# QR of P on GpSimd: reflectors in pairs in place of one at a time

## The reference

```python
U, _ = jnp.linalg.qr(P)                 # P: (144, 64), the same for all sequences
R = _rotation(cond, W, b)               # expm of a 64x64 skew matrix, one per sequence
z = jnp.einsum('btn,nd->btd', x, U)
z_rot = jnp.einsum('btd,bde->bte', z, R)
x_rot = x + jnp.einsum('btd,nd->btn', z_rot - z, U)
```

## Time and profile before

| | |
|---|---|
| median of three executions | 1263.58 us |
| profiled execution, span from first to last instruction | 1267.7 us |
| TensorE busy | 1194.4 us, 94% |
| VectorE busy | 910.0 us, 72% |
| ScalarE busy | 788.0 us, 62% |
| GpSimd busy | 749.6 us, 59%, 2230 instructions |
| mean granted TensorE clock | 0.974 |

### The profile page before, as it was taken

How to read it: one execution, slowest core, us unless ns; L and a number is a source line. 1 busy time by engine, 2 the same in 40 slices (tenths; PEclk the granted TensorE clock), 3 DMA queues, 4 the chain that set the end, 5 groups by cost and what they waited for, 6 DMA issues and landing times.

```text
span 1267.7 us, 35439 instructions
## 1 busy us (share of the span) xinstructions
PE 1194.4 (94%) x12778; PEld 949.3 (75%) x12778; DVE 910.0 (72%) x2496; ACT 788.0 (62%) x1809; POOL 749.6 (59%) x2230
## 2 busy tenths in 40 slices
PE   4899999899899999999999999999899999999997
PEld 2677777688676777778888888887777777777775
DVE  6799999766579999965575555554679999955432
ACT  3589898756479898963342333233379888874531
POOL 5656656666656656566676666667777777740000
PEclk9999999999979999999999999999969999989997
DMA  6321121242531121130210111120121111101130
GB/s 171 62 19 19 18 23 16 48 97 33 107 67 20 15 21 16 21 57 5 16 14 5 16 15 7 13 44 20 35 43 27 31 35 33 23 6 20 19 66 28
DMA packets 50319, 42.82 MB, mean 34 GB/s; under 512 B 8455, under 2 KB 45754, under 8 KB 49717
## 3 DMA queue, kind: packets, MB, share of 16 engines
q1 hardware_dynamic: 45884, 29.91, 10.9%
q0 software_dynamic: 3488, 8.52, 8.4%
q10 hardware_dynamic: 780, 2.17, 0.5%
HBM read 33.86 MB, written 3.03 MB: 29 GB/s over the span
## 4 chain that ended last, share of the span: by engine, by line
PE 82%; DVE 13%; issue 4%; ACT 2%; DMA 0%; SPq 0%; ACTq 0%; DVEq 0%
PE PS L1678 18%; PE PSA L1399 15%; PE PSA L1456 8%; PE PS L1480 8%; PE PS L1441 7%; PE PS L1399 6%; DVE BIG L544 3%; PE PSB L1651 2%; PE PS L1511 2%; PE PS L1501 2%; PE PS L1512 2%; PE PSB L1463 1%; PE PS L1506 1%; PE PS L1491 1%; DVE xh L508 1%
## 5 line engine op out<-in xcount | busy, mean ns | idle before, releaser
L1255 ACT ACTIVATE BIG<-PSA 128x512 f32<-128x512 f32 (+1 forms) x224 | 132.0, 593 | 264.1 <-PE PSA L1399 264.0
L1678 PE MATMUL PS<-w,BIG 128*128 128x144 f32 (+1 forms) x1920 | 254.7, 287 | 7.6 <-DVE BIG L818 4.1
L544 DVE TENSOR_REDUCE BIG<-PSA 128x8 f32<-128x1024 f32 x192 | 234.1, 1219 | 31.9 <-PE PSA L1456 29.9
L1678 PEld LDWEIGHTS PS<-w,BIG 128*128 128x128 f32 (+1 forms) x1920 | 245.1, 190 | 15.6 <-DVE BIG L818 4.9
L1124 ACT ACTIVATE BIG<-PSB 128x1024 f32<-128x1024 f32 x192 | 195.5, 1018 | 20.5 <-PE PSB L1463 20.3
L1456 PEld LDWEIGHTS PSA<-KK,Q 32*128 32x128 f32 x1536 | 109.9, 196 | 57.8 <-issue 41.0
L1456 PE MATMUL PSA<-KK,Q 32*128 32x128 f32 x1536 | 135.1, 294 | 14.9 <-DVE BIG L544 4.7
L1441 PE MATMUL PS<-K,qt 128*128 128x128 f32 x768 | 127.3, 293 | 10.4 <-DVE qt L539 4.8
L1463 PE MATMUL PSB<-Q,KK 32*128 32x128 f32 x1536 | 133.9, 293 | 0.0
L1480 PE MATMUL PS<-BIG,VA 128*32 128x128 f32 x3072 | 128.5, 287 | 1.1 <-DVE col L419 1.1
L1893 POOL MEMSET qprod<- 128x2 f32 x63 | 6.2, 99 | 203.0 <-DMA VB<-QA 203.0
(11 more groups left out here) (307 smaller groups left out, 2955.8 us busy)
## 6 DMA issues: line engine op xcount, KB each, us to landing
gate<-gates SPq DMA_DIRECT2D x96, 72.0 KB, 2.9
mgate<-gates SPq DMA_DIRECT2D x96, 72.0 KB, 2.7
VB<-skew POOLq DMA_DIRECT2D x16, 288.0 KB, 3.7
X<-in_x SPq DMA_DIRECT2D x4, 576.0 KB, 11.4
out<-X SPq DMA_DIRECT2D x8, 288.0 KB, 3.6
BIG<-in_skew_w SPq DMA_DIRECT2D x2, 1024.0 KB
w<-in_w SPq DMA_DIRECT2D x1, 1440.0 KB, 11.4
BIG<-in_wqkv SPq DMA_DIRECT2D x2, 584.0 KB
```

Source lines behind the costliest of these rows:

```text
L544: V.tensor_reduce(nmax.rearrange("p (s w) -> p s w", w=HP)[:, 2 * a:2 * a + 2, 3 * HD:3 * HD + G], PSA[:, :].rearrange("p (r g k) -> p r g ...
L1255: S.activation(hm[0:rows, slot, :], PS[(par * FTOT[l] + j) % 2][0:rows, :], gelu).then_inc(gelu_done, 1)
L1678: last = mm(o, hm[0:rows, slot, s * 128:(s + 1) * 128], w2[0:rows, FT * e + k, :], start=(k == 0), stop=(k == FT - 1))
```

## The change

Reflectors are made two at a time. `reflect_first(k)` broadcasts rows k and k + 1 together (two DMAs, one wait) into two buffers that lie behind `QA`, so that an instruction can run over two or three of the rows at once. It forms three sums in one tree of the same eight levels: QA times row k, row k times itself, row k + 1 times row k. With them it applies reflector k to `QA` and to the broadcast copy of row k + 1 in one subtraction. `reflect_second(k + 1)` then needs no broadcast: the copy is up to date. The one-column instructions are regrouped to run over two or three neighbouring scalars, and small values (TINY) stand where zeros stood. On the way back `unreflect` takes two rows: three sums in one tree (UT times either row, row times row), a correction for the second factor, and two subtractions. The tree lives in two buffers instead of seven. The rest of the kernel is as it was.

```diff
+            def add_up(product, n):
+                a = product
+                for size, t in ((72, qtree), (36, qtwo), (18, qtree), (9, qtwo), (4, qtree), (2, qtwo[:, 32:64]), (1, qtree)):
+                    t = t[:, 0:n * size].rearrange("p (n c) -> p n c", n=n)
+                    link(R.tensor_tensor(t, a[:, :, 0:size], a[:, :, size:2 * size], ALU.add))
...
+                link(R.tensor_tensor(qs[:, 0:n].rearrange("p (n o) -> p n o", o=1), a, nine[:, :, 8:9], ALU.add))
...
             def broadcast(k):
-                rows_in[k % 2] += 16
-                row = QA[k:k + 1, k:C].rearrange("p (o n) -> p o n", o=1).broadcast_to([1, 128, C - k])
-                pool.dma_start(QB[k % 2][:, k:C], row).then_inc(q_row[k % 2], 16)
+                for j in range(2):
+                    row = QA[k + j:k + j + 1, k:C].rearrange("p (o n) -> p o n", o=1).broadcast_to([1, 128, C - k])
+                    pool.dma_start(reach[:, 1 + j, k:C], row).then_inc(q_row, 16)
...
+            def signed_root(k):
+                link(R.tensor_tensor(norm, sq, qc[:, 0:1], ALU.pow))
+                link(R.tensor_scalar(qsn[:, k:k + 1], side, -1.0, norm, ALU.add, ALU.mult))
...
+            def kept_factors(k):
+                R.tensor_scalar(qtau[:, k:k + 1], first[:, 1:2], SMALL, qtau[:, k:k + 1], ALU.is_gt, ALU.mult)
+                R.tensor_scalar(qtau[:, k + 1:k + 2], second[:, 1:2], SMALL, qtau[:, k + 1:k + 2], ALU.is_gt, ALU.mult)
...
+            def mixed(k, to, n, step):
+                span = slice(0, 3, step)
+                link(R.tensor_tensor(to, reach[:, span, k], qsn[:, k:k + 1].broadcast_to([128, n]), ALU.mult))
+                link(R.tensor_tensor(to, to, qs[:, 0:n], ALU.add))
+                R.tensor_tensor(to[:, 0:1], to[:, 0:1], qmask[:, k:k + 1], ALU.mult)
+                link(R.tensor_tensor(qtau[:, k:k + 1], to[:, 1:2], qc[:, 1:2], ALU.pow))
...
+            def reflect_first(k):
                 broadcast(k)
                 if k:
-                    R.memset(qprod[:, :, k - 1:k], 0.0)
...
+                    kept_factors(k - 2)
+                    R.memset(products[:, :, k - 2:k], TINY)
+                pool.wait_ge(q_row, 32 * (k // 2 + 1))
+                v = reach[:, 1, :]
+                R.tensor_tensor(products[:, 1:3, k:C], reach[:, 1:3, k:C],
+                                v[:, k:C].rearrange("p (o n) -> p o n", o=1).broadcast_to([128, 2, C - k]), ALU.mult)
+                link(R.tensor_tensor(products[:, 0, k:C], QA[:, k:C], v[:, k:C], ALU.mult))
...
+                signs(k, v)
+                add_up(products, 3)
+                signed_root(k)
+                mixed(k, first, 3, 1)
+                at = slice(k + 1, C)
+                R.tensor_scalar(products[:, 0, at], v[:, at], first[:, 0:1], qtau[:, k:k + 1], ALU.mult, ALU.mult)
+                link(R.tensor_scalar(products[:, 2, at], v[:, at], first[:, 2:3], qtau[:, k:k + 1], ALU.mult, ALU.mult))
+                link(R.tensor_tensor(reach[:, 0:3:2, at], reach[:, 0:3:2, at], products[:, 0:3:2, at], ALU.subtract))
...
+            def reflect_second(k):
+                v = reach[:, 2, :]
+                R.memset(products[:, 0:2, k - 1:k], TINY)
+                R.tensor_tensor(products[:, 1, k:C], v[:, k:C], v[:, k:C], ALU.mult)
+                link(R.tensor_tensor(products[:, 0, k:C], QA[:, k:C], v[:, k:C], ALU.mult))
+                signs(k, v)
+                add_up(products[:, 0:2], 2)
+                signed_root(k)
+                mixed(k, second, 2, 2)
...
+            for k in range(0, RD, 2):
+                reflect_first(k)
+                if k == RD - 2:
+                    pool.wait_ge(sk_ld, 32)
+                    pool.dma_start(v_rows, QA[0:RD, :]).then_inc(v_st, 16)
+                reflect_second(k + 1)
...
+            def unreflect(k, vb, j):
+                v = vb[:, j * C:(j + 2) * C].rearrange("p (n c) -> p n c", n=2)
+                at, n = slice(k, C), C - k
+                R.tensor_tensor(back[:, 0:2, at], v[:, :, at], UT[:, at].rearrange("p (o n) -> p o n", o=1)
+                                .broadcast_to([128, 2, n]), ALU.mult)
+                link(R.tensor_tensor(back[:, 2, at], v[:, 0, at], v[:, 1, at], ALU.mult))
+                add_up(back, 3)
+                link(R.tensor_scalar(side, qs[:, 2:3], qs[:, 1:2], qtau[:, k + 1:k + 2], ALU.mult, ALU.mult))
+                R.tensor_scalar(back[:, 1, at], v[:, 1, at], qs[:, 1:2], qtau[:, k + 1:k + 2], ALU.mult, ALU.mult)
+                link(R.tensor_tensor(norm, qs[:, 0:1], side, ALU.subtract))
+                link(R.tensor_scalar(back[:, 0, at], v[:, 0, at], norm, qtau[:, k:k + 1], ALU.mult, ALU.mult))
+                link(R.tensor_tensor(UT[:, at], UT[:, at], back[:, 1, at], ALU.subtract))
+                link(R.tensor_tensor(UT[:, at], UT[:, at], back[:, 0, at], ALU.subtract))
```

More of the change, by code:

```diff
@@ L43 @@
 K_N = K_LOW + NE * NE
-FWD, BWD = 15, 6
+TINY, SMALL = 1e-37, 1e-30
 RADD = bass.bass_isa.ReduceOp.add
@@ L1855, in _ @@
             pool.wait_ge(q_at, 1)
-            steps, rows_in = [2], [0, 0]
+            steps = [2]
             def link(ins):
@@ L1884, in _ @@
[L1884 to L1889, removed]
+            link(R.tensor_scalar(qmask, K[:, K_SGN:K_SGN + RD], 0.0, None, ALU.is_lt))
+            qtwo = QU[:, :, :].rearrange("p n c -> p (n c)")
+            def add_up(product, n):
[3 more added lines that the diff above has]
+                    link(R.tensor_tensor(t, a[:, :, 0:size], a[:, :, size:2 * size], ALU.add))
+                    if size == 9:
+                        nine = t
+                    a = t
+                link(R.tensor_tensor(qs[:, 0:n].rearrange("p (n o) -> p n o", o=1), a, nine[:, :, 8:9], ALU.add))
@@ new lines, in _ @@
+            reach = qrows[:, 2 * C:5 * C].rearrange("p (n c) -> p n c", n=3)
+            products = VB[1][:, 0:3 * C].rearrange("p (n c) -> p n c", n=3)
+            sq, side, norm, first, second = qs[:, 1:2], qs[:, 3:4], qs[:, 4:5], qs[:, 5:8], qs[:, 8:10]
+            def broadcast(k):
+                for j in range(2):
+                    row = QA[k + j:k + j + 1, k:C].rearrange("p (o n) -> p o n", o=1).broadcast_to([1, 128, C - k])
+                    pool.dma_start(reach[:, 1 + j, k:C], row).then_inc(q_row, 16)
@@ new lines, in reflect_first @@
+                link(R.tensor_tensor(reach[:, 0:3:2, at], reach[:, 0:3:2, at], products[:, 0:3:2, at], ALU.subtract))
[8 more added lines that the diff above has]
+                mixed(k, second, 2, 2)
+                if k == RD - 1:
+                    kept_factors(k - 1)
+                    return
+                at = slice(k + 1, C)
+                link(R.tensor_scalar(products[:, 0, at], v[:, at], second[:, 0:1], qtau[:, k:k + 1], ALU.mult, ALU.mult))
+                link(R.tensor_tensor(QA[:, at], QA[:, at], products[:, 0, at], ALU.subtract))
@@ L1929, in _ @@
+            NG = RD // VG
+            pool.wait_ge(v_st, 16)
             load_group(NG - 1)
             load_group(NG - 2)
+            link(R.memset(qrows[:, 0:3 * C], 0.0))
             for g in reversed(range(NG)):
@@ L1933, in _ @@
                 pool.wait_ge(v_ld[g % 2], 16 * ((NG - 1 - g) // 2 + 1))
-                link(R.tensor_copy(vb[:, k0:k0 + (VG - 1) * (C + 1) + 1:C + 1], qdiag[:, k0:k0 + VG]))
-                for j in reversed(range(VG)):
-                    unreflect(k0 + j, vb[:, j * C:(j + 1) * C])
+                pivots = vb[:, k0:k0 + (VG - 1) * (C + 1) + 1:C + 1]
+                R.memset(vb[:, C + k0:C + k0 + 2 * (C + 1) + 1:2 * (C + 1)], 0.0)
+                link(R.tensor_tensor(pivots, pivots, qsn[:, k0:k0 + VG], ALU.add))
+                for j in reversed(range(0, VG, 2)):
+                    unreflect(k0 + j, vb, j)
                 if g >= 2:
```

58 lines of the change are left out of this document (16 added, 42 removed).

## The result

The kernel after takes 1275.65 us in the median, the kernel before 1266.62 in the runs beside it (nine each; the 1263.58 that the prediction is set against was the median of the first three). The ratio is 1.0075, 95% interval 1.0048 to 1.0101: about 9 us slower. The profiled execution took 1280.35 us with a span of 1278.2.

The account below looks back on a forecast made before the run. The prediction took the TensorE and VectorE chain to bound the kernel, not GpSimd. VectorE's burden, 3.8 us saved and 1.9 added, netted -1.9; half reaching the end gave -1.0 from 1263.58, so 1262.6 us, range 1258.4 to 1267.

Parts of the forecast that it names:

- What bounds the kernel: Chain of TensorE 82% and VectorE 13%, without GpSimd; U is ready 15.3 us before it is read.
- The price of the pairs: GpSimd's QR: 21.7 us a pair forward against 25.9, 7.3 back plus 1.5 a group; U ready near 970 us.
- the bounds given: Last write of UT: right if between 900 and 1040 us.
- What the earlier end is worth: VectorE's burden in the three attentions: 3.8 us saved, 1.9 added, net -1.9; about half reaches the end, -1.0 us.
- a factor of 1.3: First two attentions: burden follows squared GpSimd durations over time, 2.9 in 12.97 to 6.3 in 21.7; 6.2 us grows by 1.9.
- The read part is the "slower" rival's rule: First two attentions: only duration above 0.2 us blocks, squares grow by 2.2; +7.4 against -3.8 us, 1267.2; chance 0.13.
- the credit: Third attention: GpSimd works only 45 of 200 us, so 3.8 of VectorE's 4.8 us burden go.
- The step from excess to time: About half of VectorE's time change reaches the end, as VectorE waits for TensorE at times.
- The faster one: Passage from third attention to its MLP: TensorE's clock doesn't fall, 7 us of work take 3.5; 1257.6 us, chance 0.22.
- The range: Whole kernel: 1258.4 to 1267 us, from near the faster rival to the slower one.
- the added fall of the clock: First passage, with the slower rival: a further fall of the clock would add 3.4 us.
- The 0.2% that the prediction said a measurement can tell: Whole kernel: a measurement can tell about 0.2%, 2.5 us, from no change.

Follow-up runs that it names:

- The streams: In place of the QR, GpSimd repeats one instruction of fixed width: products of 16, 72, 144 or 288 columns, or memsets; ratios to before 0.9971 to 1.1765.
- the single forward part and the new way back: Kernel after with the forward part one reflector at a time, in the new buffers, the way back still in pairs; ratio to before 1.0089.
- 72 columns: No QR; in its place GpSimd does 2150 products of 72 columns from two SBUF inputs; ratio to before 1.0081.
- the 144 column stream: No QR; in its place GpSimd does 1600 products of 144 columns from two SBUF inputs; ratio to before 1.0501.
- the wide stream: No QR; in its place GpSimd does 1130 products of 288 columns from two SBUF inputs; ratio to before 1.1765.
- the pause: Kernel after with one GpSimd wait, 63 us long, ahead of group 9 of the way back; ratio to before 1.0064.
- the kernel with all split: Kernel after with row instructions over 100 columns halved, tree levels in pieces of at most 72 columns, trees shrunken; 1266.0 us against before's 1265.55, ratio 0.9993.
- the one with new forward part and single back: Kernel after with the way back one reflector at a time, in the new buffers, the forward part still in pairs; ratio to before 1.0045.

## Why the prediction was wrong

**What bounds the kernel: right.** U was not waited for, before or after, and nothing of its earlier end was worth time.

**The price of the pairs: right in kind.** U is complete at 1016 us, not near 970, within the bounds given. The two landings together wait 142.1/32 = 4.4 us and not 3.2, and a pair takes 23.8 us forward and not 21.7; more than half of that is the landing. Back, a pair with its share of the group's work takes 7.7 us, where 258/32 = 8.1 was reckoned. So U's delay against 970 comes from the forward part, which ended at 770 and not at 708.

**"What the earlier end is worth": the step that failed.** The prediction summed VectorE's burden over the three attentions alone and so put the MLPs at nothing; there it rose most. It also booked a saving in the third attention that did not come. The matched excess by stage, us:

| stage | before | after |
|---|---|---|
| first attention | 3.6 | 3.2 |
| first MLP | 3.1 | 4.1 |
| second attention | 3.0 | 3.8 |
| second MLP and the passages beside it | 7.7 | 18.9 |
| third attention | 4.4 | 6.5 |
| from 60 us to the end | 21.8 | 36.5 |

Three terms, the second the largest.

First, the size of the squares. The prediction took whole durations, 2.9 to 6.3 us squared per step, and a factor of 1.3 for their density. The streams show that only the read part counts. With it the factor is 62.4/33.7 = 1.85 over the whole run; the excess grew by 35.2/20.0 = 1.76, while the whole durations of the same instructions, squared, grew only from 276 to 306 us squared. In the first two attentions, where the prediction used its factor, the error was small: S doubled (10.4 to 20.3), and the matched excess was 6.6 us before and 7.0 after. Over the three kernels with a single forward part its mean is 5.6 us, over the three with the new one 8.9: 3.3 more, where the prediction had 1.9. The read part is the "slower" rival's rule, which put 2.2 on the forward part alone; it had 0.13, held back by the earlier trace rows, where VectorE's busy time doesn't follow GpSimd's. That comparison hid the burden. Without the QR VectorE is busy 180.50, 180.50 and 180.30 us in the same windows, so before's third shows only 1.2 us more, where the matched excess of the stage is 4.4: with TensorE at 1.2 GHz until 941 us, that window holds 452 of VectorE's instructions and not 463. A kernel without the QR was not at hand then.

Second, the place. Only attentions were counted. The second layer's MLP has 128 gated sums with two SBUF inputs, and the way back, without the landing waits that thin out the forward part, now falls on it: the matched excess there, with the passages beside it, rose by 11.2 of the 14.7 us in all. S in these stretches went from 8 to 22.

Third, the credit. Of the third attention's 4.8 us 3.8 were to be saved. GpSimd worked in it until 1016, not 970, with its widest instructions, and the matched excess rose from 4.4 to 6.5 us.

The step from excess to time, about half, was near: 15.2 us of excess gave 9 of time, 0.6 of it. Against the kernel without a QR the shares are 0.2 (before), 0.4 (after and 72 columns), 0.6 (144) and 0.9 (288): the share grows with the burden. That VectorE's slack is used up is one reason, argued and not shown. TensorE's clock is another: the profiled execution without a QR spends 32 us at 1.2 GHz, the one beside the 144 column stream 96 and the one beside the wide stream 219. At half speed the difference is worth up to 32 of some 68 us and up to 94 of some 228, as an estimate, and no run separates the two. For the pairs the clock can't be the whole: with the single forward part and the new way back, and with the pause, the mean granted clock is 0.977 and 0.976, against 0.978 and 0.976 for before beside them. The nine executions of after have 0.972, so a part of its own 9 us may be the clock.

**The rivals.** The slower one came true in kind: it reckoned 3.6 us net (+7.4 in two attentions, -3.8 in the third), where 9 came, mostly from the MLPs and without the credit. The faster one's clock did go as it said at the third passage. The windows of the kernel after:

```profile
276.00:283.00 7.00, 5.73 (x21) 5.38 (x22) 2.90 (x9) 1.84 (x4) 5.78 (x15) 0.51 0.01 2
931.60:941.60 10.00, 8.86 (x72) 6.58 (x74) 8.06 (x22) 7.10 (x14) 8.14 (x25) 0.50 0.36 83
1109.00:1116.00 7.00, 6.83 (x119) 5.28 (x117) 6.62 (x19) 6.73 (x20) 0.00 (x0) 1.00 0.07 14
```

The clock is 1.00 where it was 0.51, and 2.6 us came back there. A stretch of 6.8 us at 1.2 GHz from 276 us on is new; the 3.6 us lost around 260 to 280 lie there. GpSimd's absence isn't shown to be the cause: the kernel with all split has GpSimd at work until 1113 and no low stretch there either, the one with new forward part and single back has none at work after 1047 and a low one.

**The range** ended at 1267.0; the slower rival with the added fall of the clock was stated to lie outside, and the unseen MLP lies beyond it too. Slower had a chance of 0.15, and the reason given for it was the attentions; the MLP was in no rival.

## What to carry to other kernels

Work on GpSimd that nobody waits for still costs time through VectorE's SBUF operands. The cost goes about with the square of the width of GpSimd's instructions, so fusing two rows into one instruction saves GpSimd 0.2 us and, by that law, doubles what the pair costs VectorE. Where GpSimd has slack, split: at 100 columns or fewer, with smaller trees, the loss was gone here. To price it, sum the squares of the read parts over the whole run, all stages, take one run without GpSimd's work as zero, and compare instruction by instruction, since a window fixed in time holds other work in each kernel.

## What the runs showed of the hardware

**The block is the read part.** I had not expected the fixed 0.2 us of an instruction to be free to VectorE: 3100 instructions of 16 columns, with GpSimd busy for 742 us, cost 5.4 us of VectorE's time and no measurable time. The rule of the Trainium skill quoted in the prediction (SBUF — State Buffer, Who interferes with whom) has the whole instruction exclude; the streams show 584 of 834 ns at 288 columns and 5 of 239 at 16, and the measurement decides.

**The clock's stretches scatter.** The runs of before in one comparison went from 1254.94 to 1272.43 us. Two profiled kernels with the same S differ in these stretches. Before (windows; columns as in the earlier trace rows):

```profile
345.00:365.00 20.00, 18.79 (x152) 13.93 (x151) 12.31 (x31) 12.34 (x25) 12.13 (x34) 0.50 0.55 135
919.00:941.00 22.00, 21.96 (x195) 16.73 (x192) 15.79 (x46) 15.75 (x30) 17.09 (x59) 0.50 0.25 50
```

and the kernel with single reflectors both ways:

```profile
351.00:366.00 15.00, 13.03 (x206) 9.38 (x200) 13.27 (x40) 13.58 (x32) 10.08 (x32) 1.00 0.39 73
931.00:941.00 10.00, 9.19 (x138) 7.07 (x139) 8.60 (x21) 8.63 (x20) 7.84 (x27) 1.00 0.10 31
```

Before stays at 1.2 GHz for 20.5 us from 344.5 and 23.9 us from 917.9; the other for 6.8 and 17.1. Their spans are 1267.7 and 1257.0 us, and their medians can't be told apart. The 0.2% that the prediction said a measurement can tell was too fine: the intervals above are ±0.3% for a ratio of many runs, and a single execution tells less still. Differences of a few us between two traces are believed here only where several kernels showed them.
